# Two of eight probability slots of six attention units, transposed by DMA moves and VectorE squares

## What is computed

```python
hn = group_norm(x, gn1_scale, gn1_bias)
qkv = jnp.einsum('bchw,oc->bohw', hn, w_qkv) + b_qkv[None, :, None, None]
q, k, v = jnp.split(qkv.reshape(b * NHEAD, 3 * ch, n), 3, axis=1)
scale = ch ** (-0.25)
wgt = jnp.einsum('bct,bcs->bts', q * scale, k * scale)
wgt = jax.nn.softmax(wgt, axis=-1)
a = jnp.einsum('bts,bcs->bct', wgt, v).reshape(b, c, h, w)
out = jnp.einsum('bchw,oc->bohw', a, w_proj) + b_proj[None, :, None, None]
return x + group_norm(out, gn2_scale, gn2_bias)
```

## Time and profile before

| | |
|---|---|
| runs, median (lowest to highest) | 3433.38 us (3432.56 to 3433.63) |
| profiled execution, its own time | 3435.15 us |
| its span, first to last instruction | 3433.4 us |
| PE busy | 3384.5 us, 99% |
| DVE busy | 2113.5 us, 62% |
| ACT busy | 1833.5 us, 53% |
| POOL busy | 1063.5 us, 31% |
| `transposes`, 4096 instructions (L571) | 551.4 us busy |
| moves of layer 1 (L444), 256 DMAs of 128 KB | median 2.4 us to landing |

### The profile page before, as it was taken

How to read it: one execution, slowest core, us unless ns; L and a number is a source line. 1 busy time by engine, 2 the same in 40 slices (tenths; PEclk the granted TensorE clock), 3 DMA queues, 4 the chain that set the end, 5 groups by cost and what they waited for, 6 DMA issues and landing times.

```text
span 3433.4 us, 51840 instructions
## 1 busy us (share of the span) xinstructions
PE 3384.5 (99%) x16816; PEld 2774.2 (81%) x16816; DVE 2113.5 (62%) x3452; ACT 1833.5 (53%) x3082; POOL 1063.5 (31%) x947
## 2 busy tenths in 40 slices
PE   7999999999999999999999999999999999999999
PEld 4788888888888888887878878888788888888887
DVE  4577456774577735776357854578545784557744
ACT  3578226772278622785237843378333882347822
POOL 1245113441034420444104531145211452114511
PEclk9999999999999999999999999999999999999999
DMA  7522235222443125341253312542224422343212
GB/s 308 165 45 63 92 112 147 48 52 92 133 126 85 40 85 148 95 99 53 65 172 78 84 74 57 159 97 64 77 74 139 99 62 92 81 138 77 62 56 74
DMA packets 109849, 332.10 MB, mean 97 GB/s; under 512 B 21744, under 2 KB 54768, under 8 KB 98800
## 3 DMA queue, kind: packets, MB, share of 16 engines
q1 hardware_dynamic: 109552, 328.45, 33.6%
HBM read 162.68 MB, written 31.49 MB: 57 GB/s over the span
## 4 chain that ended last, share of the span: by engine, by line
PE 89%; DVE 3%; DMA 3%; ACT 2%; SPq 1%; issue 1%; POOL 0%; ACTq 0%; DVEq 0%; POOLq 0%
PE big L471 25%; PE big L598 13%; PE ops L584 13%; PE tps L571 13%; PE big L668 7%; PE tps L739 5%; PE big L636 5%; PE ops L739 4%; PE ops L471 3%; DMA ST<-ST 1%; SPq L387 1%; DMA d_m<-PT 1%; ACT PB L854 1%; DMA d_u<-ST 1%; PE ops L709 0%
## 5 line engine op out<-in xcount | busy, mean ns | idle before, releaser
L994 POOL TENSOR_SCALAR PB<-PB,small 128x1024 f32<-128x1024 f32 x576 | 648.3, 1126 | 1314.2 <-DVE small L1224 1302.9
L1218 DVE TENSOR_REDUCE small<-big 128x1 f32<-128x1024 f32 x512 | 625.2, 1221 | 99.1 <-PE big L598 95.8
L1229 DVE TENSOR_TENSOR PT<-tps,PT 128x512 fp32r<-128x512 f32 x1024 | 652.3, 679 | 32.5 <-ACT PT L860 32.1
L860 ACT ACTIVATE PT<-tps 128x512 fp32r<-128x512 f32 x1024 | 566.8, 597 | 146.8 <-PE tps L571 144.2
L854 ACT ACTIVATE PB<-big,small 128x1024 f32<-128x1024 f32 x512 | 572.7, 1119 | 100.0 <-DVE small L1218 97.0
L584 PE MATMUL ops<-PT,VT 128*128 128x512 f32 x2048 | 599.1, 414 | 0.0
L598 PE MATMUL big<-ST 128*128 128x512 f32 x2048 | 555.0, 393 | 9.5 <-DMA ST<-ST 9.5
L571 PEld LDWEIGHTS tps<-ident,PB 128*128 128x128 f32 x4096 | 467.3, 140 | 116.5 <-DVE PT L1229 55.3
L571 PE MATMUL tps<-ident,PB 128*128 128x128 f32 x4096 | 551.4, 275 | 8.8 <-DVE PT L1229 6.1
L598 PEld LDWEIGHTS big<-ST 128*128 128x128 f32 x2048 | 383.1, 188 | 97.6 <-issue 12.0
L584 PEld LDWEIGHTS ops<-PT,VT 128*128 128x128 f32 x2048 | 346.1, 189 | 47.2 <-DVE PT L1229 5.0
(11 more groups left out here) (158 smaller groups left out, 4785.1 us busy)
## 6 DMA issues: line engine op xcount, KB each, us to landing
ST<-ST SPq DMA_DIRECT2D x384, 256.0 KB, 5.0
W<-d_qk SPq DMA_DIRECT2D x32, 1024.0 KB, 6.2
W<-PB SPq DMA_DIRECT2D x256, 128.0 KB, 2.4
XA<-in_x SPq DMA_DIRECT2D x8, 2048.0 KB, 7.6
X<-in_x SPq DMA_DIRECT2D x8, 2048.0 KB, 10.6
W<-d_wp SPq DMA_DIRECT2D x8, 2048.0 KB, 12.0
W<-d_g SPq DMA_DIRECT2D x8, 2048.0 KB, 12.0
W<-d_m SPq DMA_DIRECT2D x8, 2048.0 KB, 7.8
```

What stands on the lines that cost most here:

```text
L860: act_fn(pt_slot(u, s)[:, 0, :], tps[n % 2][:], ACT.Copy).then_inc(s_pt_hi, 1)
L994: nc.gpsimd.tensor_scalar(PB[:, i, :], PB[:, i, :], rinv[:, i:i + 1], 1.0, ALU.mult, ALU.mult)\
L1218: V.tensor_reduce(negmax[:, i:i + 1], tile(("s", 4 * u + tb))[:], axis=AX.X, op=ALU.max, negate=True).then_inc(s_row_max, 1)
L1229: V.tensor_tensor(pt_slot(u, s)[:, 1, :], tps[n % 2][:], pt_slot(u, s)[:, 0, :].bitcast(f32), ALU.subtract).then_inc(s_pt_ready, 1)
```

## The change

Units 0, 1, 4, 5, 8 and 9 (`MOVED`, the first two units of the pairs 0 to 2) get their slots 6 and 7 (`MOVED_SLOTS`, 12 of the 128 slots of a batch) by another way than PE:

- `exps` of a moved unit writes `PB` in another order: in every 256 columns the two slots stand interleaved, word by word. PE's transposes of such a unit's slots 0 to 5 read every second word.
- SP: `move_quarters(u)` waits until the unit is normalised (`s_p_norm`) and until the squares of the moved unit before have been read (`s_squared`), then issues 16 DMAs of 32 partitions x 4 x 64 words, from `PB` into `X[:, 0, :]`. It stands ahead of the `stack_head` calls of the next pair.
- DVE: at the end of step 4u + 7, `square(6)` and `square(7)`: two transposes of 32x32 squares from `X[:, 0, :]` into `X[:, 2, :]`, the first behind a wait for the 16 moves.
- ACT and DVE: `pt_hi` and `pt_lo` of the two slots read `X[:, 2, :]` instead of `tps`. `pt_hi` gets two waits, for the square and for the slot of `PT` to be free (`s_slot_free`, raised by PE in `values0`).
- PE: no `transposes` for the two slots. The waits on `s_pt_ready` are unchanged.
- The load of x moves from the start of the attention to behind the third pair's last moved unit (`s_pt_ready` at 80), ahead of the load of `W[0]`; `scale_x` stands behind `normalise` 50, 52, 54 and 56.

```diff
+def moved_units(pairs):
+
+    return [u for pair in range(pairs) for u in (4 * pair, 4 * pair + 1)]
+
+
+MOVED = moved_units(PAIRS - 1)
+MOVED_SLOTS = [8 * u + s for u in MOVED for s in (NT - 2, NT - 1)]
...
-X_SCALE_STEPS = (20, 23, 26, 29)
+X_SCALE_STEPS = (50, 52, 54, 56)
...
 
+        F0 = X[:, 0, :].rearrange("p (q t n) -> p q t n", q=QUARTERS, t=KB)
+
+        def squared(s):
+
+            return X[:, 2, HALF * (s % 2):HALF * (s % 2) + HALF]
+
+        def t_count(b, n):
+
+            return b * (8 * UNITS0 - len(MOVED_SLOTS)) + len([m for m in range(n + 1) if m not in MOVED_SLOTS])
+
+        def squared_count(b, n):
+
+            return b * len(MOVED_SLOTS) + MOVED_SLOTS.index(n) + 1
+
+        def moved_count(b, u):
+
+            i = MOVED.index(u)
+            return (b * (len(MOVED) // 2) + i // 2 + 1) * EXCHANGE
...
+        s_moved = [sem("moved_even"), sem("moved_odd")]
+        s_squared = sem("squared")
+        s_slot_free = sem("slot_free")
...
+                def move_quarters(u):
+                    half = u % 2
+                    sp.wait_ge(s_p_norm, b * 72 + 4 * u + 4)
+                    own_wait(sp)
+                    if u:
+                        sp.wait_ge(s_squared, squared_count(b, 8 * MOVED[MOVED.index(u) - 1] + NT - 1))
+                    own_wait(sp)
+                    for tq in range(QUARTERS):
+                        for sq in range(QUARTERS):
+                            sp.dma_start(F0[32 * sq:32 * sq + 32, tq, :, :],
+                                         PB[32 * tq:32 * tq + 32, 4 * half:4 * half + 4,
+                                            6 * P + 64 * sq:6 * P + 64 * sq + 64]).then_inc(s_moved[half], 16)
+
                 sp.wait_ge(s_out_done, (b * 8 + CREDIT) * 16)
                 own_wait(sp)
-                sp.dma_start(X[:], src_x(b)).then_inc(s_x_res, 16)
                 sp.wait_ge(s_v_full, b * 4 + 4)
                 own_wait(sp)
+                move_quarters(0)
                 for i in (2, 3):
                     sp.dma_start(w_qk(i).rearrange("p h k n -> p (h k n)").bitcast(f32), d_qk[i]).then_inc(ld_qk[i], 16)
+                move_quarters(1)
                 stack_head(b, 1, 0)
                 sp.dma_start(W[1][:].bitcast(f32), d_wp[:]).then_inc(s_ld_wp, 16)
                 stack_head(b, 1, 1)
+                move_quarters(4)
+                move_quarters(5)
                 stack_head(b, 2, 0)
                 stack_head(b, 2, 1)
+                move_quarters(8)
+                move_quarters(9)
                 stack_head(b, 3, 0)
+                sp.wait_ge(s_pt_ready, b * 144 + 80)
+                own_wait(sp)
+                sp.dma_start(X[:], src_x(b)).then_inc(s_x_res, 16)
                 sp.dma_start(W[0][:].bitcast(f32), d_g[:]).then_inc(s_ld_g, 16)
                 stack_head(b, 3, 1)
                 sp.wait_ge(s_big_full, big_count(b, ("proj", KB - 1)))
...
                     if n >= 2:
                         pe.wait_ge(s_pt_ready, b * 144 + n - 1)
                     for t in range(4):
-                        last = nc.tensor.transpose(tps[n % 2][:, P * t:P * t + P],
-                                                   PB[:, 4 * (u % 2) + t, P * s:P * s + P], ident[:])
+                        row = PB[:, 4 * (u % 2) + t, :]
+                        if u in MOVED:
+                            keys = row[:, 2 * P * (s // 2):2 * P * (s // 2) + 2 * P].rearrange("p (k s) -> p s k", s=2)[:, s % 2, :]
+                        else:
+                            keys = row[:, P * s:P * s + P]
+                        last = nc.tensor.transpose(tps[n % 2][:, P * t:P * t + P], keys, ident[:])
                     last.then_inc(s_t_full, 1)
 
                 def values0(n):
...
                     if s == 7:
                         last.then_inc(s_o_full, 1)
+                    elif n + 4 in MOVED_SLOTS:
+                        last.then_inc(s_slot_free, 1)
 
...
                     if last_values(step):
                         project_last_v(last_values(step))
                     if n >= 0:
-                        transposes(n // 8, n % 8)
-                        transposes(n // 8, n % 8 + 1)
+                        for m in (n, n + 1):
+                            if m not in MOVED_SLOTS:
+                                transposes(m // 8, m % 8)
...
                     t = full(("s", 4 * u + tb))
                     act.wait_ge(s_row_max, b * 64 + 4 * u + tb + 1)
                     i = 4 * (u % 2) + tb
-                    act_fn(PB[:, i, :], t[:], ACT.Exp, bias=negmax[:, i:i + 1], accum_out=rowsum[:, i:i + 1])\
+                    to, scores = PB[:, i, :], t[:]
+                    if u in MOVED:
+                        to = to.rearrange("p (h q r s) -> p h s q r", h=4, q=QUARTERS, s=2)
+                        scores = scores.rearrange("p (h s q r) -> p h s q r", h=4, q=QUARTERS, s=2)
+                    act_fn(to, scores, ACT.Exp, bias=negmax[:, i:i + 1], accum_out=rowsum[:, i:i + 1])\
                         .then_inc(s_exp_done, 1)
 
                 def pt_hi(u, s):
                     n = 8 * u + s
-                    act.wait_ge(s_t_full, b * 128 + n + 1)
-                    act_fn(pt_slot(u, s)[:, 0, :], tps[n % 2][:], ACT.Copy).then_inc(s_pt_hi, 1)
+                    if n in MOVED_SLOTS:
+                        act.wait_ge(s_squared, squared_count(b, n))
+                        act.wait_ge(s_slot_free, squared_count(b, n))
+                        turned0 = squared(s)
+                    else:
+                        act.wait_ge(s_t_full, t_count(b, n))
+                        turned0 = tps[n % 2][:]
+                    act_fn(pt_slot(u, s)[:, 0, :], turned0, ACT.Copy).then_inc(s_pt_hi, 1)
 
...
                 def pt_lo(u, s):
                     n = 8 * u + s
                     dve.wait_ge(s_pt_hi, b * 144 + n + 1)
-                    V.tensor_tensor(pt_slot(u, s)[:, 1, :], tps[n % 2][:], pt_slot(u, s)[:, 0, :].bitcast(f32),
+                    turned0 = squared(s) if n in MOVED_SLOTS else tps[n % 2][:]
+                    V.tensor_tensor(pt_slot(u, s)[:, 1, :], turned0, pt_slot(u, s)[:, 0, :].bitcast(f32),
                                     ALU.subtract).then_inc(s_pt_ready, 1)
+
+                def square(n):
+                    u, s = n // 8, n % 8
+                    if s == 6:
+                        dve.wait_ge(s_moved[u % 2], moved_count(b, u))
+                    V.transpose(squared(s).rearrange("p (t q r) -> p t q r", t=KB, q=QUARTERS),
+                                F0.rearrange("p q t (r s) -> p s t q r", s=2)[:, s - 6, :, :, :])\
+                     .then_inc(s_squared, 1)
 
...
                     if n >= 0:
                         pt_lo(n // 8, n % 8)
                         pt_lo(n // 8, n % 8 + 1)
+                    for m in (n + 2, n + 3):
+                        if m in MOVED_SLOTS:
+                            square(m)
```

## The result

The change made the kernel slower: median 3506.95 us (3502.91 to 3510.69, 4 runs) against 3433.51 us of before, a ratio of 1.0215 (95% interval 1.0201 to 1.0229), or +73 us. The forecast was 3478 us, range 3420 to 3500: the direction was right, the size too small by 29 us, and the time lies outside the range.

A forecast was written before the change was run, and what follows sets the result against it. PE (TensorE), 99% busy, was taken to bound the kernel. Each pair of units was to gain 0.4 us and lose 2.25, +1.85 us, 24 times: +44 us, giving a forecast of 3478 us, range 3420 to 3500.

The forecast's parts named there:

- What is removed: Eight transposes per step on PE, 0.91 us; 48 groups, 43.7 us, the gain if nothing else ended last.
- what DVE gains: Two squares at the end of step 4u+7 take 1.2 us on DVE, which has nothing idle there.
- Even units: Units 0, 4, 8, scores of step 9: the later exp of step 8 lets only 0.4 of 0.91 us be kept.
- Odd units and the port: Units 1, 5, 9, step 13: PE waits for pt_lo, delayed by squares and the port shared with POOL; 2.25 us lost.
- the rival in which DVE keeps the port: Step 12: DVE's second pt_lo goes ahead of POOL's head_out; a pair loses 0.6 us, 3448 us; chance 0.19.
- signs of being wrong: DVE waits long for the moves, transposes take over 0.91 us a group, or PE doesn't wait in step 13.
- The moves: Sixteen DMAs taking 12.9 us land 0.4 us before DVE's squares need them, so they cost nothing.
- x later: The later load of x adds at most 10.6 us ahead of the last stack moves, still in time: no cost.
- Strided access: Exps writing and transposes reading every second word: at most 0.13 us per exp, off the path; no cost for PE reads.
- Late moves: Rival: moves land 2 us later than in layer 1, 48 us more, 3526 us; chance 0.06.
- slow strided reads: Rival: PE's remaining transposes slow down, up to 131 us on top of 44, 3609 us; chance 0.03.
- The faster one: Rival: squares delay DVE less than they take, turning at 0.94 us; 3420 us at a 0.6 us delay; chance 0.16.

The follow-up runs named there:

- e1_even: The change with only units 0, 4 and 8 moving their slots, not 1, 5 and 9: 3425.15 us, ratio 0.9976 to the kernel before.
- e8_even_corr: On top of e6_even_exp, ScalarE also does its corr ahead of exps in the moved units' step: 3416.11 us, ratio 0.9949 to the kernel before.
- e4_twice: The change with PE computing the scores of steps 13, 29 and 45 twice, ahead of its wait: 3478.29 us, ratio 1.0132 to before.
- e3_head: The change with POOL's head_out waiting until the two moved slots' low halves are done: 3454.19 us, ratio 1.0060 to before.
- e2_tps: The change with transposes waiting only for the low half of the slot that last held their tps buffer: 3472.46 us, ratio 1.0115 to before.
- e6_even_exp: On e1_even, squares placed behind row_max and recip, and exps ahead of the two pt_hi: 3427.28 us, ratio 0.9981 to the kernel before.
- e9_tps_head: The change with the edits of e2_tps and e3_head together, all six units moved: 3447.22 us, ratio 1.0039 to the kernel before.

## Why the prediction was right in sign and too small

- **What is removed, what DVE gains.** Right. Without the group of step 12 PE came to the scores of step 13 0.94 us sooner (0.91 forecast). The squares took 1.22 us (1.2 forecast), and DVE had no gap for them.
- **Even units.** Right in mechanism, sized too well: 0.4 us forecast, 5.3 / 24 = 0.22 us measured, 0.09 us of strided transposes taken off. On the mean of the batches the scores of step 9 came 0.62 us sooner behind those of step 8, those of steps 25 and 41 0.43, and all lost 0.2 us in the step behind. In e1_even, where unit 1 isn't moved, the same stretches gain 9.8 / 24 = 0.41 us, as forecast. The wait was the forecast one: the scores waited for `exps`, and where `exps` comes first, in e8_even_corr, they come 0.94 us sooner. This costs the sum 4.3 us.
- **Odd units and the port.** Right. 2.25 us were forecast; 2.0 us came of it in each of the 24 where the clock is left out (e4_twice). The second `pt_lo` takes 1011.98 - 1010.23 = 1.75 us, and `head_out` goes ahead of it. e3_head shows the port's share, 1.08 us. So it went by the forecast, and not by the rival in which DVE keeps the port. The Trainium skill ("SBUF — State Buffer", "SBUF: two separate sides") has whoever starts first hold the pair for its whole instruction; the rows agree, since `head_out` asked while the first `pt_lo` ran and went next. This term was 6.1 us too large.
- **The step that failed: PE's wait was costed at its length alone.** The text read the granted clock (1.00) and then put the odd unit's wait into the sum at its length alone (the 2.25 us). Behind it TensorE fell to 1.2 GHz in 17 of 24 odd units: 25.7 us, of an excess of 29 (3506.95 measured, 3478 forecast). The term is missing from the sum and from every rival; with it the forecast would have been about 3504 us. That the rest comes out is luck: the even units gain 4.3 us less and the odd ones lose 6.1 us less than forecast, the rest of layer 0's attention adds 3.9 us, and what lies outside it takes off 2 us. The Trainium skill ("TensorE: Matmul & The Clock Gate", "HAM oscillation — how this bites in real kernels") describes such a fall behind longer waits, for DMAs: PE goes back to half clock, and the next stretch of products begins slow. The rows agree on the slow stretch, with 0.79 as the mean of such a step, but here it came behind waits of 1.45 and 1.02 us, shorter than those that the Trainium skill gives there. That the clock may fall should have been a rival, and of the signs of being wrong that the prediction names none looks at the clock.
- **Costed at nothing.** The moves: right, the squares never waited for them. x later: nearly right, 0.19 x 8 = 1.5 us stand at step 58, where `normalise` 55 is late; in turn the scores of step 30 come 0.27 us sooner in e1_even, as `scale_x` no longer stands behind `normalise` 26 (a cause that is not shown by a run). Strided access: wrong by a little. It cost 0.07 to 0.09 us in some three groups of each pair of units, by estimate 24 x 0.25 = 6 us, spread over even, odd and rest. The row that I took (0.114 us a transpose, from 0.91 / 8) was that of a group that waits; without a wait it is 0.79 / 8 = 0.099 us, and there is room to be slower. The Trainium skill ("SBUF — State Buffer", "Specifications (TRN2)") asks for two accesses to a 16-byte line for full bandwidth; a step of 8 bytes gives two, and yet the rows show 0.87 against 0.79 us.
- **The rivals.** Late moves or slow strided reads, at a part of their full price (3526 and 3609), could give the measured time too, but the rows are against them: no square waited for the moves, and a strided group is 0.08 us longer, not twice as long. The faster one failed: it needed squares that delay DVE by less than 0.94 us, and they delayed it by 1.22. That the even units alone gain has another reason, the projection behind them.

## What to carry to other kernels

Before moving work from the bound engine to another, find for each place where the other engine is idle next; the same edit won 0.2 us where a projection followed (0.8 with the order on DVE and ACT mended) and lost 2.1 to 4.7 us where none did. Price a new wait on PE twice, by its length and by the slower clock behind it. And when a wait is removed, look for what ended just ahead of it: here, in e2_tps, e6_even_exp and e9_tps_head, that was the next wait.

## What was not expected of the hardware

- TensorE's clock fell to the 1.2 GHz level behind two waits of 1.45 and 1.02 us with four transposes between them, in 17 of 24 places, and not in the other 7, where the rows ahead are alike; it didn't fall behind a single wait of 1.5 us (e3_head), or behind 0.93 and 0.67 us (e2_tps), or 0.55 and 1.02 us (e4_twice). In e4_twice it was work that is thrown away that kept it up. What decides between places that look alike no run here shows.
- Transposes that read every second word of a row are a tenth slower than those that read words in a row, 0.87 against 0.79 us for eight.
